# One core, sixteen images through edge filter, attention and a sign-weight layer: a reordered pipeline with the attention output turned on VectorE and the second key block's mask added by TensorE

## What is computed

```python
def _L0_tok_ref(x, scharr):
    gray = jnp.einsum('bchw,c->bhw', x, w)[:, None]
    edges = jax.lax.conv_general_dilated(gray, scharr, window_strides=(1, 1), padding='SAME', ...)
    return jnp.sqrt(jnp.square(edges)).sum(axis=1) / 2

def _L0_attn_ref(x, W_dq, W_uq, W_dkv, W_uk, W_uv, W_o):
    c_q = x @ W_dq
    Q = (c_q @ W_uq).reshape(Bx, Sx, N_HEADS, D_K)
    c_kv = x @ W_dkv
    K = (c_kv @ W_uk).reshape(Bx, Sx, N_HEADS, D_K)
    V = (c_kv @ W_uv).reshape(Bx, Sx, N_HEADS, D_K)
    scores = jnp.einsum('bqhd,bkhd->bhqk', Q, K) / math.sqrt(D_K)
    scores = jnp.where(causal, scores, -jnp.inf)
    attn = jax.nn.softmax(scores, axis=-1)
    out = jnp.einsum('bhqk,bkhd->bqhd', attn, V).reshape(Bx, Sx, N_HEADS * D_K)
    return out @ W_o

h = _L0_tok_ref(x, L0_tok_scharr)
h = h + _L0_attn_ref(_layernorm(h), ...)
h = h + _L0_ffn_ref(_layernorm(h), L0_ffn_weight)   # x @ sign(weight).T
```

## Time and profile before

| | us |
|---|---|
| median of 3 runs | 512.27 |
| lowest, highest | 504.1, 512.48 |
| the profiled execution | 510.29 |
| its span, first to last instruction | 508.4 |

### The profile page before, as it was taken

The page is one execution under the profiler, slowest core; times in us unless marked ns, Lnnn a source line. Parts: engine busy times, 40 slices in busy tenths (PEclk is TensorE's granted clock), DMA queues, the critical chain, the costliest instruction groups (busy, mean ns, idle before and its releaser), DMA issues.

```text
span 508.4 us, 10109 instructions
## 1 busy us (share of the span) xinstructions
PE 395.0 (78%) x3736; PEld 284.2 (56%) x3780; DVE 289.1 (57%) x508; ACT 230.7 (45%) x385; POOL 163.7 (32%) x363
## 2 busy tenths in 40 slices
PE   0047448586979898989898989898989899889863
PEld 0023335455656666666666666666666667666542
DVE  1422255574736667676666767676757576664321
ACT  2013123363635555555555555555555554446400
POOL 8220331413122424242424242424242422220111
PEclk9999569797979999999999999999999999999977
DMA  5954797675655666666767676737372425200000
GB/s 157 259 130 93 220 255 168 177 181 180 165 158 134 180 176 169 179 169 186 171 177 181 177 174 178 194 95 194 100 189 68 147 68 185 85 24 24 21 22 21
DMA packets 72186, 74.06 MB, mean 146 GB/s; under 512 B 6379, under 2 KB 65995, under 8 KB 72139
## 3 DMA queue, kind: packets, MB, share of 16 engines
q1 hardware_dynamic: 72138, 73.42, 53.6%
HBM read 51.97 MB, written 21.04 MB: 144 GB/s over the span
## 4 chain that ended last, share of the span: by engine, by line
PE 24%; POOL 23%; issue 22%; DVE 6%; ACT 1%; POOLq 0%
PE bank L771 9%; POOL parts L462 5%; POOL xn L442 4%; PE bank L764 3%; POOL yn L457 3%; PE bank L867 2%; POOL rstd L449 2%; DVE y L696 2%; PE bank L798 2%; PE bank L836 2%; POOL rstd L434 2%; DVE stats L700 1%; POOL max_rest L422 1%; POOL max_parts L427 1%; POOL max_parts L425 1%
## 5 line engine op out<-in xcount | busy, mean ns | idle before, releaser
L668 DVE TENSOR_REDUCE neg_max<-bank 128x4 f32<-128x1024 f32 x64 | 78.1, 1220 | 47.6 <-PE bank L838 46.6
L529 ACT ACTIVATE probs<-bank 128x1024 f32<-128x1024 f32 x64 | 65.6, 1025 | 63.3 <-PE bank L869 63.1
L462 POOL TENSOR_TENSOR parts<-rest,parts 128x1024 bf16<-128x1024 f32 x16 | 34.0, 2125 | 144.3 <-ACT parts L510 144.3
L784 PE MATMUL bank<-rows,band 102*32 102x256 f32 x512 | 34.3, 413 | 26.6 <-DMA rows<-gray_padded 25.7
L679 DVE TENSOR_TENSOR bank<-bank,cap_kq 128x512 f32<-128x512 f32 x64 | 44.4, 694 | 15.5 <-PE bank L886 15.5
L534 ACT ACTIVATE probs<-bank 128x512 f32<-128x512 f32 x64 | 38.2, 597 | 32.7 <-DVE bank L679 32.4
L836 PE MATMUL bank<-k_st,q_st 96*128 96x256 bf16 x256 | 48.6, 284 | 4.2 <-ACT edge L490 1.8
L867 PE MATMUL bank<-q_st,k_st 99*128 99x256 bf16 x256 | 47.5, 279 | 1.8 <-issue 0.2
L447 POOL TENSOR_SCALAR var<-mv 128x2 f32<-128x2 f32 x16 | 3.5, 219 | 133.3 <-DVE mv L704 133.3
L771 PE MATMUL bank<-w_sign,yn_t 128*128 128x256 f32 x128 | 35.1, 422 | 12.1 <-issue 9.9
L674 DVE TENSOR_REDUCE neg_max<-bank 128x4 f32<-128x512 f32 x64 | 43.6, 681 | 0.0
(11 more groups left out here) (95 smaller groups left out, 768.8 us busy)
## 6 DMA issues: line engine op xcount, KB each, us to landing
x_sb<-in_x SPq DMA_DIRECT2D x16, 768.0 KB, 6.0
rows<-gray_padded SPq DMA_DIRECT2D x48, 256.0 KB
qk_parts<-parts SPq DMA_DIRECT2D x16, 768.0 KB, 4.1
q_st<-qk_parts SPq DMA_DIRECT2D x96, 128.0 KB, 3.9
k_st<-qk_parts SPq DMA_DIRECT2D x96, 128.0 KB, 3.6
gray_padded<-gray SPq DMA_DIRECT2D x16, 258.0 KB, 3.4
out_dram<-z SPq DMA_DIRECT2D x16, 256.0 KB, 2.5
rows<-gray_padded SPq DMA_DIRECT2D x32, 24.0 KB
```

The source lines that it names most:

```text
L462: pool.tensor_tensor(parts[:, n % 2, SLOTS_OF_PART[2], :, :], rest[:, :, :, :], parts[:, n % 2, SLOTS_OF_PART[1], :, :], ALU.subtract).the ...
L529: nc.scalar.activation(probs[:, g, :, 0:S], ps_k0, ACT.Exp, scale=SCALE).then_inc(exp0_done, 1)
L668: nc.vector.tensor_reduce(neg_max[:, 1, heads], ps_hi, AX.X, ALU.max, negate=True).then_inc(max_hi_done, 1)
L784: last = nc.tensor.matmul(ps_edge[b * RB:(b + 1) * RB, t, f, :], band[0:KC, f, :], rows[0:KC, n % 2, t * (P // RB) + b, :], start=True, st ...
```

## The change

The work is put in another order on all five engines, with fewer turns (23 in place of 27), and three pieces change hands:
- `cap` goes. `key_scores_second` gets a fifth product, identity by `mask_kq` over 512 columns, and `exp_second` waits for `k1_done` alone.
- `copy_o`, `turn_output`, `turn_attn` on TensorE and `copy_at` go. In their place VectorE transposes 32x32 blocks: `turn_values` takes the 128x256 of `ps_o` out of PSUM for each group, `invert` makes the reciprocals, GpSimd's `normalize` multiplies, and VectorE's `turn_attn` transposes again, into `a_t`. The heads of a group are no longer neighbours but those of `head_of(g, i)`, so that the blocks come to lie in order.
- `sum_edges` goes from VectorE to GpSimd (`measure_h`, the statistics, stays), and the two normalizations over 256 columns go from GpSimd to ScalarE as activations with scale and bias from SBUF; `scale_x` and `scale_y` stay on GpSimd, one step of each no longer in series. `both_edges` becomes two halves.

Banks 0 to 5 are left to the scores, the edges and `ps_mt`; bank 6 takes `ps_o`, `ps_yt`, `ps_xt`, `ps_c` and half of `ps_qk`, bank 7 `ps_v`, `ps_z`, `ps_y` and the other half.

```diff
-FIRST = -6
-LAST = IMAGES + 4
+FIRST = -4
+LAST = IMAGES + 2
...
+def head_of(g, i):
+    return (g // 2) * HALF + g % 2 + 2 * i
...
@@ SyncE @@
             load_x(0)
+            load_taps()
+            clear_borders()
             load_x(1)
-            load_weights()
-            for i in range(-4, LAST + 1):
+            for i in range(FIRST, LAST + 1):
+                if live(i + 3):
+                    load_rows(i + 3)
+                if i == -3:
+                    load_projections()
+                if i == -2:
+                    load_outputs()
+                if live(i - 1):
+                    load_max_rows(i - 1, 1)
                 if live(i + 1):
                     store_parts(i + 1)
-                if live(i - 1):
-                    load_max_rows(i - 1, 1)
+                    load_operands(i + 1, 0)
+                if live(i - 3):
+                    store_z(i - 3)
+                if live(i):
+                    load_max_rows(i, 0)
                 if live(i + 4):
                     store_gray(i + 4)
                 if live(i + 6):
                     load_x(i + 6)
-                if live(i - 4):
-                    store_z(i - 4)
-                if live(i + 1):
-                    load_operands(i + 1, 0)
-                if live(i):
-                    load_max_rows(i, 0)
-                if live(i + 4):
-                    load_rows(i + 4)
                 if live(i + 1):
                     load_operands(i + 1, 1)
...
@@ GpSimd @@
+            def sum_edges(n):
+                pool.wait_ge(abs_done, T * (n + 1))
+                need(pool, y_done, upto(n - H_RING))
+                need(pool, xn_done, T * upto(n - H_RING))
+                pool.tensor_tensor(h_ring[:, n % H_RING, :, :], edge[:, :, 0, :], edge[:, :, 1, :],
+                                   ALU.add).then_inc(h_done, 1)
...
+            def normalize(n, c):
+                k = T * n + c + 1
+                pool.wait_ge(recip_done, k)
+                need(pool, at_done, k - T)
+                pool.tensor_tensor(attn[:, c, :, :, :].rearrange("p q x d -> p x q d"), u[:, c, :, :, 0:DK],
+                                   recip[:, c, :, :].unsqueeze(3).to_broadcast([P, 2, NQ, DK]),
+                                   ALU.mult).then_inc(attn_done, 1)
...
@@ ScalarE @@
+            def normalize_x(n):
+                act.wait_ge(shift_done, n + 1)
+                need(act, xt_done, n)
+                for t in range(T):
+                    nc.scalar.activation(xn[:, t, :], h_ring[:, n % H_RING, t, :], ACT.Identity,
+                                         bias=shift[:, t:t + 1], scale=rstd[:, t:t + 1]).then_inc(xn_done, 1)
...
-                act.wait_ge(capped, at + 1)
+                act.wait_ge(k1_done, at + 1)
                 nc.scalar.activation(probs[:, g, :, S:S + P], ps_k1, ACT.Exp, scale=SCALE).then_inc(exp1_done, 1)
...
@@ VectorE @@
-            def cap(n, g):
-                dve.wait_ge(k1_done, NG * n + g + 1)
-                nc.vector.tensor_tensor(ps_k1, ps_k1, cap_kq[:, :].unsqueeze(1).to_broadcast([P, G, P]),
-                                        ALU.min).then_inc(capped, 1)
...
+            def turn_values(n, g):
+                c, x = g // 2, g % 2
+                dve.wait_ge(o_done, NG * n + g + 1)
+                need(dve, attn_done, T * (n - 1) + c + 1)
+                nc.vector.transpose(u[:, c, x, :, :].rearrange("p q d -> p (q d)"), ps_o).then_inc(o_turned, 1)
...
+            def turn_attn(n, c):
+                dve.wait_ge(attn_done, T * n + c + 1)
+                need(dve, proj_done, n - 1)
+                nc.vector.transpose(a_t[:, n % 2, c, :],
+                                    attn[:, c, :, :, :].rearrange("p q x d -> p (q x d)")).then_inc(at_done, 1)
...
@@ TensorE @@
-                    last = nc.tensor.matmul(ps_k1[:, i, :], k[:, hh, P:S], q[:, hh, P:S],
-                                            start=True, stop=True)
-                last.then_inc(k1_done, 1)
+                    hh = head_of(g, i)
+                    nc.tensor.matmul(ps_k1[:, i, :], k[:, hh, P:S], q[:, hh, P:S],
+                                     start=(i == 0), stop=False, skip_group_check=True)
+                nc.tensor.matmul(ps_k1[:, :, :], ident_bf[:, :], mask_kq[:, :, :], start=False, stop=True,
+                                 skip_group_check=True).then_inc(k1_done, 1)
...
             def values(n, g):
                 pe.wait_ge(exp1_done, at + 1)
-                need(pe, o_copied, at)
+                need(pe, o_turned, at)
+                if g == 0:
+                    need(pe, yt_copied, upto(n - 2))
+                if g == 1:
+                    need(pe, xt_copied, upto(n + 3))
+                if g == 2:
+                    need(pe, c_copied, upto(n + 3))
+                if g == 3:
+                    need(pe, rest_done, 2 * upto(n + 3))
...
             def feed_forward(n):
                 pe.wait_ge(yt_copied, n + 1)
-                need(pe, max_hi_done, NG * upto(n + 3) + (1 if live(n + 4) else 0))
-                need(pe, abs_done, upto(n + 6))
-                need(pe, y_done, upto(n))
+                need(pe, v_copied, upto(n + 4))
```

More of the change, by code:

```diff
@@ L430, in normalize_x, with draw_diagonals @@
-            def normalize_x(n):
+            def draw_diagonals():
+                for dx in range(TAPS):
+                    if dx:
+                        pool.wait_ge(drawn, dx)
+                    part = diag[dx * RB:(dx + 1) * RB]
+                    pool.affine_select(out=part, in_=part, compare_op=ALU.not_equal, fill=1.0,
+                                       base=0, pattern=[[-1, TAPS], [-1, RB]],
+                                       channel_multiplier=1).then_inc(drawn, 1)
+                for dx in range(TAPS):
+                    pool.wait_ge(drawn, TAPS + dx)
+                    foot = diag[FOOT:P]
+                    pool.affine_select(out=foot, in_=foot, compare_op=ALU.not_equal, fill=1.0,
+                                       base=TAPS * RB - dx, pattern=[[-TAPS, TAPS], [-TAPS, RB]],
+                                       channel_multiplier=1).then_inc(drawn, 1)
+                pool.wait_ge(drawn, 2 * TAPS)
@@ L503, in first_part @@
                 need(act, parts_out[n % 2], 16 * (n // 2))
-                for i in range(2):
-                    act.wait_ge(qk_done, 2 * n + i + 1)
-                    nc.scalar.copy(parts[:, n % 2, 4 * i, :, :], ps_qk[:, i, :, :]).then_inc(part0_done, 1)
+                act.wait_ge(qk_done, n + 1)
+                for i in (1, 0):
+                    nc.scalar.copy(parts[:, n % 2, 4 * i, :, :], ps_qk[i]).then_inc(part0_done, 1)
             def second_part(n):
@@ L984, in _ @@
                 if live(i - 1):
-                    key_scores_first(i - 1, 1)
+                    values(i - 1, 0)
+                if i == 0:
+                    pe.wait_ge(signed, 1)
+                    pe.wait_ge(v_copied, 2)
+                    turn(ps_w, signs, turned)
+                if live(i - 3):
+                    feed_forward(i - 3)
                 if live(i + 2):
-                    compress(i + 2)
+                    turn_x(i + 2)
                 if live(i - 1):
-                    key_scores_second(i - 1, 1)
-                if live(i - 3):
-                    project(i - 3)
-                if live(i - 2):
-                    values(i - 2, 3)
+                    key_scores_first(i - 1, 2)
+                    key_scores_second(i - 1, 2)
                 if live(i):
@@ L998, in _ @@
                 if live(i - 1):
-                    key_scores_first(i - 1, 2)
+                    values(i - 1, 1)
                 if live(i - 2):
-                    turn_output(i - 2, 0)
-                if live(i - 1):
-                    key_scores_second(i - 1, 2)
-                    values(i - 1, 0)
-                if live(i + 2):
-                    expand_qk(i + 2)
+                    project(i - 2)
                 if live(i):
                     turn_max(i, 0)
+                if i == -2:
+                    pe.wait_ge(up_ready, 1)
+                    pe.wait_ge(weights_in, 4 * 16)
+                if live(i + 2):
+                    compress(i + 2)
+                if live(i - 1):
+                    key_scores_first(i - 1, 3)
+                    key_scores_second(i - 1, 3)
                 if live(i):
```

478 lines of the change are left out of this document (208 added, 270 removed).

## The result

| | before | after |
|---|---|---|
| median of 4 runs, us | 510.48 | 457.5 |
| lowest, highest | 504.1, 512.48 | 455.05, 457.77 |
| the profiled execution | 510.29 | 457.7 |
| its span | 508.4 | 455.8 |

The ratio is 0.902, 95% interval 0.894 to 0.911: faster, by 53 us between the medians and by some 50 by the ratio. Forecast: 452, range 434 to 484.

What follows compares the result with a forecast made beforehand. Before was taken as bound by a loop of waits through GpSimd's order, TensorE next; fill 59, turns 89.3 + 210.6 + 56.9 and drain 34 gave 449.8 us of span, plus 1.9: 451.7, forecast 452, range 434 to 484.

Steps and rivals of the forecast that it cites:

- What bounds before: Steady turn of before: a loop of waits through GpSimd's fixed order sets 25.8 us, TensorE next, 2.9 us below.
- TensorE's sum of 22.6 us without waits: TensorE's steady turn: 25.8 less 2.5 of waits, less 1.6 of transposes, plus 0.9 of mask products.
- New waits, 0.5 + 0.2 + 0.1: TensorE each turn: values for the rests 0.5 us, filters for max_hi 0.2, four other groups together 0.1.
- The turn of 23.4 us: Steady turn after the change: TensorE's 22.6 us of work plus its new waits.
- rival 1: The loop only moves: maxima rows land after 6.0 us behind operands and z, 25.6 us a turn, 480 us; chance 0.21.
- The way through DRAM, s + 23.0: Third part, parts store, loads, first-half maxima rows: landing 23.0 us after turn start s, just inside 23.4.
- The other engines as cover: VectorE about 15.9 us a turn, ScalarE 14.3, GpSimd no more than before, hidden under TensorE save the DRAM stretch.
- The mask: Second key block's mask on TensorE: four products of 512 columns, 0.22 us each, 0.9 us a turn.
- Fill 59: Start to first scores: filters start at 21 us, then 38 us more, 59 in all (52 to 66).
- Turns 0 to 3, 89.3: First four turns: 20 us for turn 0, held by DRAM without maxima, then 22.5, 23.4 and 23.4.
- Turns 4 to 12, 210.6; 13 to 15, 56.9: Nine steady turns of 23.4 us; then 21.5, 18.4 and 17 as filters and later pieces of work fall away.
- Drain 34: After the last image: 13 us for the last keys' turn, then a serial path of 21, its projection at 5.4.

Runs made afterwards that it cites:

- before_second_early: The kernel before with one ScalarE piece, second_part(i+2), moved ahead of the exponentials of group 3 and both_edges: 488.2 us, ratio 0.965.
- rows_later: The changed kernel with SyncE issuing load_max_rows(i-1, 1) ahead of load_rows(i+3): 450.43 us, ratio 0.891.
- rows_fill: The changed kernel with load_max_rows(i-1, 1) ahead of load_rows(i+3) from turn 1 on, the old order in the fill: 448.49 us, ratio 0.882.
- the control: The changed kernel as it is, run again beside before: 454.72 us, ratio 0.899.
- cap_back_rows: The changed kernel with the second mask on VectorE as before, plus the load order of rows_fill: 443.77 us, ratio 0.872.
- parts_in_halves: z_behind with the parts stored in two halves of heads, each with its own semaphore: 436.4 us, ratio 0.860.
- z_behind: cap_back_rows with the store of z issued behind the first half's maxima rows: 440.84 us, ratio 0.866.
- cap_back: The changed kernel with the second mask on VectorE as a minimum again, its four mask products gone from TensorE: 455.13 us, ratio 0.900.
- norms_on_pool: The changed kernel with both 256-column normalizations on GpSimd again, SyncE's order unchanged: 466.75 us, ratio 0.918.

## Why the prediction was right, point by point

- *What bounds before* (the loop through GpSimd, TensorE next): shown by `before_second_early`. One moved call gave 23 us by the medians, 18 by the ratio.
- *TensorE's sum of 22.6 us without waits*: right, with two small misses that cancel. The 22.91 of the earlier trace rows lacks records; with all of them TensorE's work went from 23.10 (`before_second_early`) to 22.59 (`rows_later`). With 0.9 for four mask products, the three sets of transposes were 1.4, where 1.6 was taken, and before stood for 2.7 us, where 2.5 was taken. The short turn of 22.98 holds the 22.6, 0.26 for the rests and 0.1 more.
- *New waits, 0.5 + 0.2 + 0.1*: sized too large. `values` waited 0.26 us for the rests, and the filters for `max_hi` once in the execution (1.3 us). TensorE's side of it was right (3.4 us from the end of the filters); the second rest is read 3.5 us after that end and not 3.95, because ScalarE's instructions overlap a little: the two halves of `normalize_y` take 1.08 us together, and begin 0.1 us before the second half of the edges has ended. The Trainium skill (ScalarE: Activation LUTs, What ACT_TABLE_LOAD costs) gives 186 ns and 0.833 for each column, and some 93 more for each pointer operand, from which 585 ns is an estimate for 256 columns with two pointers. The normalizations on ScalarE took 590 and 593 ns, so the trace agrees. 0.6 was the right value to take.
- *The turn of 23.4 us*: right as a number (23.3 in the mean), partly for another reason. Five of nine are 22.98 or 22.99, the others 23.3 to 24.1. The long ones come from rival 1's mechanism at a place I hadn't named: not the first half's rows behind operands and z, but the second half's behind operands and `load_rows`. I had put no `load_rows` into the way of any maxima row, though SyncE's new order shows it directly ahead of `load_max_rows(i - 1, 1)`; "ahead in the queue" was costed for the issue and not for the bytes. The landing of 5.9 us is at the far end of the bounds used for the first half (2.5 to 6.0). It cost 0.3 us a turn and not 2.2, because only four of the nine turns have `load_rows` close enough ahead, and each loses 1.1 us at most: `rows_fill` against the control is 6 us, most of it in turns 0 to 3; rival 1 had 28. That these turns kept to the forecast's 23.4 is in part luck: the waits that were taken came to 0.3 instead of 0.8, and a wait that had no term brought 0.3.
- *The way through DRAM, s + 23.0*: not the bound in after, and the walk was too slow in its first half: in the turn whose first key scores start at 268.73, the third part ended at s + 9.9 (predicted 11.1), and the first half's rows were issued at s + 18.5 (19.6). It came into the chain as soon as TensorE was relieved (`cap_back_rows`), and of the two cuts made from it `parts_in_halves` gave time and `z_behind` likely did.
- *The other engines as cover*: right. VectorE 15.7 us (15.9), ScalarE 14.2 (14.3), GpSimd 9.7, though its sum of 512 columns takes 1.27 us where 1.06 was taken. A transpose of 128x256 on VectorE took 450 ns from PSUM and 415 from SBUF, where 420 was taken.
- *The mask* was costed at 0.9 us on TensorE and that its place on VectorE is cover. Shown: of the parts that were tried it is the one that loses. Alone it makes before slower by 3 to 5 us, and taking it back on top of `rows_fill` gains 4.7; in after's own order taking it back makes no difference, since the late rows eat what it returns.
- *Fill 59*: 58.4. Two misses cancel: the filters start at 22.5 us instead of 21, and the rest takes 35.8 instead of 38.
- *Turns 0 to 3, 89.3*: 94.0, the largest miss. The step "turn 0: 20 us, turn 1: 22.5" failed; they took 23.8 and 24.6. The chain of after shows it:

```profile
66.24 7.50 DMA qk_parts<-parts
...
86.44 6.62 DMA q_st<-top_rows
```

The store of the parts lands after 7.5 us instead of the 4.1 taken; then SyncE issues from 73.75 almost without a pause to 86.4, `load_rows` last, and the rows of turn 1 land 6.6 us later. The DMA share is 0.75 here, against 0.66 before. In `rows_fill`, whose store in turn 0 takes 8.1 us, turn 0 still takes 23.2, but turn 1 takes 20.8 and the four together 88.8: so the slow store is the miss of turn 0, and the maxima rows behind `load_rows` that of turn 1. `parts_in_halves` took another 3.4; how much of that is the store and how much the relieved TensorE wasn't separated.
- *Turns 4 to 12, 210.6; 13 to 15, 56.9*: 209.7 and 56.9. The second is luck in its parts: 22.4, 18.1 and 16.5 us, where 21.5, 18.4 and 17 were taken.
- *Drain 34*: 36.8. The step "values and `feed_forward(14)` to the projection at 5.4" failed. From the y of image 14 the chain runs serially (below it the window of its feed-forward):

```profile
430.28 0.70 DVE y L723
...
434.08 0.59 ACT yn L580
...
436.06 3.52 PE bank L806 x8
...
440.41 1.98 PE bank L806 x8
```

```profile
430.28:436.00 5.72, 3.22 (x46) 2.00 (x45) 3.58 (x10) 3.18 (x5) 1.94 (x5) 0.98 0.00 0
436.00:440.40 4.40, 3.52 (x8) 2.54 (x9) 0.69 (x1) 0.00 (x1) 0.00 (x0) 0.64 0.00 0
```

The projection of image 15 at 440.4 stands behind `feed_forward(14)`, which waits 5.8 us for its own layer norm and then needs 3.52 us where it has 1.99 in the steady turns. The granted clock is 0.64 in the mean under it, between its two levels, and was 0.98 in the 5.7 us before, in which TensorE was busy 3.2. The prediction had the low clock in the last feed-forward only. That is 10.1 us instead of 5.4; the turn before it took 11.3 instead of 13.

Where the 53 us came from, as far as it was shown: 23 are opened by the earlier second part alone (18 by the ratio, in before's own surroundings), 14 are the transposes off TensorE. They need not add up with the rest, since each was measured beside another limit. The mask takes back nothing in after's order, and the late rows take back 4 (`rows_later`) to 6 (`rows_fill`). The rest isn't shown: the shorter pipeline may account for much of it (11 us lie in the drain), but neither it nor the sum of edges on GpSimd was run by itself.

## What to carry to other kernels

When a loop of waits bounds a kernel, look for the one call in an engine's order that stands ahead of the loop's next link: here one move without any new instruction was worth over a third of what the whole change gave. Before you weigh what an edit gives back to an engine, make sure that this engine is the limit in every turn: `cap_back` looked worthless until one 12 KB transfer had been issued ahead of 0.8 MB of others, and then the same edit gained 5 us. In a hand-written queue, cost a small transfer by the bytes ahead of it, not by its own. And before you take a difference of two busy times for the work that was moved, compare the counts of their records: here four records a turn were missing, which made 0.5 us.

## What the runs showed of the hardware

A DMA of 12 KB landed 5.8 to 6.6 us after its issue where the last of `load_rows`' 0.8 MB had been issued at most 1.5 us before it (after and `norms_on_pool`), which is longer than the store of 768 KB took in the median (4.4 us). Behind six operand loads and the store of z it took 3.7 us once and 2.3 once (282.05 and 260.37 in `cap_back_rows`).

GpSimd's small casts and differences of 16 columns take 0.20 to 0.22 us, but 0.64 and 0.67 where VectorE runs its two gray operations (after's timeline, GpSimd, then VectorE):

```profile
278.91 0.22 POOL L455 TENSOR_TENSOR top_rest<-top,top_parts 128x16 f32<-128x16 f32 x1
279.19 0.64 POOL L458 CAST top_parts<-top_rest 128x16 bf16<-128x16 f32 x1
279.91 0.67 POOL L460 TENSOR_TENSOR top_parts<-top_rest,top_parts 128x16 bf16<-128x16 f32 x1
```

```profile
279.08 0.69 DVE L670 SCALAR_TENSOR_TENSOR gray<-x_sb,gray 128x512 f32<-128x512 f32 x1 [0.55 <-ACT gray L516]
279.81 0.69 DVE L673 SCALAR_TENSOR_TENSOR gray<-x_sb,gray 128x512 f32<-128x512 f32 x1
```

Each ends within 0.1 us of the VectorE operation that it overlaps, and so it is in each of the eleven turns of after that show such a pair. The Trainium skill (SBUF — State Buffer, Who interferes with whom) says that a VectorE instruction with two SBUF inputs contends with a GpSimd one that reads SBUF, for ports that only one of them can hold at a time. The trace agrees, at 0.4 us for each of the two. No run here moved them apart.
